# A long network on one core: the pair mask and the conditioning vectors computed inside the expert stage, spline tables in one 128-row stack, zeroing issued at the start

## The reference, cut to what matters

```python
x = x + L0_gnn(layernorm(x), src, dst, ...)    # edge messages, summed over the edges of a node
x = x + L0_ffn(layernorm(x))                   # 64 experts with spline tables, one expert for each node
x = x + L1_gnn(layernorm(x), edge_index, node_vec1, ...)  # 4 blocks of attention over the edges
x = x + L1_ffn(layernorm(x))
```

```python
h = einsum('nd,nhd->nh', xf, Wd[tidx]);  hn = sigmoid(h);  idx = clip(int(hn * 16), 0, 15)
hs = spline_bases[tidx][..., idx] + spline_slopes[tidx][..., idx] * (hn * 16 - idx)
y = einsum('nh,ndh->nd', hs, Wu[tidx]) * scale[tidx]
```

```python
ph = noise_levels * freqs                       # 32 frequencies
cond = silu(concat([sin(ph), cos(ph)]) @ f_w1 + f_b1) @ f_w2 + f_b2    # 16 values for each node
```

## Time and profile before

| | us |
|---|---|
| median of the runs | 3249.67 (3 runs, 3239.88 to 3250.24) |
| the profiled execution | 3248.55 |
| its span in the trace | 3246.8 |

### The profile page before, as it was taken

One profiled execution on the slowest core, in us unless ns is written; L12 is line 12 of the kernel. 1 busy time (PEld: TensorE's weight loads), 2 busy tenths in 40 slices (PEclk: granted clock), 3 DMA queues, 4 the chain that ended last, 5 costly groups with the idle time before them and its releaser, 6 DMA issues. The chain is left out here.

```text
span 3246.8 us, 39720 instructions
## 1 busy us (share of the span) xinstructions
PE 2617.4 (81%) x13663; PEld 2223.8 (68%) x13663; DVE 1904.5 (59%) x3591; ACT 1358.5 (42%) x2707; POOL 1107.7 (34%) x826
## 2 busy tenths in 40 slices
PE   3999998358870178998889988989978999773999
PEld 3688886247670067886678876868866789653997
DVE  1899997624605445776536765457655467625762
ACT  1556664300351234664336653346543356412431
POOL 2788886856701001223103231022311122322520
PEclk9999999668595579999899998999999999985999
DMA  7444442167157411103211012121022210223101
GB/s 223 90 84 78 85 80 52 9 185 186 13 204 201 135 38 48 40 9 95 91 41 56 16 56 88 61 55 40 29 83 78 61 32 17 83 84 89 51 20 32
DMA packets 182808, 245.03 MB, mean 75 GB/s; under 512 B 110073, under 2 KB 118708, under 8 KB 175247
## 3 DMA queue, kind: packets, MB, share of 16 engines
q1 hardware_dynamic: 95852, 213.89, 22.7%
q0 software_dynamic: 86752, 28.51, 5.3%
HBM read 188.85 MB, written 52.95 MB: 74 GB/s over the span
## 5 line engine op out<-in xcount | busy, mean ns | idle before, releaser
L2108 POOL TENSOR_SCALAR prob<-prob,rden,linked 125x1250 f32<-125x1250 f32 x160 | 223.9, 1399 | 959.9 <-DVE rden L2075 959.9
L581 POOL DMA_INDIRECT pairs<-late_cnt,late_idx x160 | 348.0, 2175 | 115.5 <-issue 68.3
L2026 ACT CAST prob_high<-ps 125x375 fp32r<-125x375 f32 (+1 forms) x480 | 231.3, 504 | 266.5 <-PE ps L1988 266.2
L2067 DVE CUSTOM_DVE_ANT_0 prob<-ps,mask 125x1250 f32<-125x1250 f32 x160 | 233.1, 1457 | 128.1 <-PE ps L1964 113.0
L2080 DVE TENSOR_TENSOR prob_low<-ps,prob_high 125x375 fp32r<-125x375 f32 (+1 forms) x480 | 269.7, 585 | 46.6 <-ACT prob_high L2026 46.6
L340 POOL DMA_INDIRECT Hg<-h_rows,dsti x160 | 232.2, 1451 | 102.3 <-issue 82.4
L1977 PE MATMUL ps<-ident,prob 125*125 125x125 f32 x1600 | 252.3, 273 | 17.3 <-POOL prob L2108 10.7
L1977 PEld LDWEIGHTS ps<-ident,prob 125*125 125x125 f32 x1600 | 232.3, 187 | 29.8 <-POOL prob L2108 22.9
L540 PE MATMUL ps<-onehot,mhi 125*128 125x512 f32 (+1 forms) x960 | 245.7, 364 | 6.3 <-DVE onehot L428 5.7
L540 PE MATMUL ps<-onehot,mlo 125*128 125x512 f32 (+1 forms) x960 | 238.5, 357 | 0.0
L2018 ACT ACTIVATE prob<-prob,top 125x1250 f32<-125x1250 f32 x160 | 214.6, 1341 | 44.4 <-DVE top L2067 35.9
(11 more groups left out here) (396 smaller groups left out, 6066.1 us busy)
## 6 DMA issues: line engine op xcount, KB each, us to landing
mask<-mask_d SPq DMA_DIRECT2D x40, 546.9 KB
g_row<-g_d SPq DMA_DIRECT2D x80, 250.0 KB
g_d<-g_row SPq DMA_DIRECT2D x70, 250.0 KB
sg_wd<-L_ffn_Wd SPq DMA_DIRECT2D x32, 512.0 KB
w_ring<-L_ffn_Wd SPq DMA_DIRECT2D x16, 1024.0 KB, 5.3
w_ring<-L_ffn_Wu SPq DMA_DIRECT2D x16, 1024.0 KB, 4.9
pairs<-zeros POOLq DMA_DIRECT2D x18, 625.0 KB, 17.7
keyrow<-keys_d SPq DMA_DIRECT2D x40, 244.1 KB
```

Source lines behind the costliest of these rows:

```text
L581: nc.gpsimd.indirect_dma_start(pairs[a][:, :], bass.IndirectOffsetOnAxis(T.E.late_idx[:, c:c + 1], 0), T.E.late_cnt[:, c:c + 1], None, com ...
L2026: s.copy(M.pt[0][:, n % 3, 0:w], T.ps[0:P, 3 + n % 4, 0:w]).then_inc(high, 1)
L2067: v.tensor_tensor_reduce(M.prob[:, r, :], S(u)[0:P, 0:N], M.mask[:, it % MASKS, :], 1.0, 3.0e38, ALU.add, ALU.min, M.top[:, r:r + 1]).then ...
L2108: nc.gpsimd.tensor_scalar(M.prob[:, r, :], M.prob[:, r, :], M.rden[:, r:r + 1], T.linked[:, it:it + 1], ALU.mult, ALU.mult).then_inc(norme ...
```

## The change

- `pair_mask` and `condition` are no stages any more; their work is written into the lists of `experts`.
- The conditioning: loads by SP behind the tables' load; angles by DVE between down blocks 13 and 25; transposes on PE after down block 34, products after blocks 42 and 56; ACT's part after the rounding of the tables.
- The pair mask: loads and stores are issued by POOL, after the last pair add and after `hs_ready` has reached its last tile; POOL's gathers of `y_d` come behind them. DVE makes the ten tiles after the look-up, with one `tensor_tensor_reduce` in place of the addition and the maximum. ACT takes the logarithms of tiles 0 to 6 after up blocks 12, 20, ... 60, and those of tiles 7 to 9 after the copies of the out phase. Those ten copies are now all ACT's. Two buffers as before.
- The tables: loaded twice, into rows 0 to 63 and 64 to 127. Rows 0 to 63 keep the rounded part, rows 64 to 127 become the rest. `R.hot` has 128 rows with both halves alike (`route` makes them with one more small product), so that a chunk takes 2 matmuls. The last picks of a tile are three over both tables in place of six.
- The zeros are issued without waiting for `x` and the edge inputs.

The diff, cut to its core:

```diff
@@ input_projection, POOL
                     nc.gpsimd.memset(ones33[:], 1.0).then_inc(cleared, 1)
-                    pool.wait_ge(x_in, 32)
-                    pool.wait_ge(e_in, 160)
                     for a in pairs:
@@
+LN0, LNSTEP, LNS = 12, 8, 7
@@ route, PE / ACT / DVE
+                    pe.wait_ge(sec_ready, 1)
+                    pe.wait_ge(doubled, 2)
+                    mm(T.ps[:, 7, 0:4], twice[:].rearrange("p a e -> p (a e)"), sec[:], start=True, stop=True).then_inc(ends_made, 1)
+                    for k in range(2):
+                        nc.scalar.copy(twice[:, k, :], T.ident[0:NX, 0:NX]).then_inc(doubled, 1)
-                    do(v.tensor_scalar(lo_ok[:], T.iota_n[0:NX, :], sec[:, 0:1], None, ALU.is_ge))
+                    dve.wait_ge(ends_made, 1)
+                    do(v.tensor_copy(ends[:], T.ps[:, 7, 0:4]))
+                    do(v.tensor_scalar(lo_ok[:], T.iota_n[:], ends[:, 0:1], None, ALU.is_ge))
@@ experts, SP
-                    sp.dma_start(raw.rearrange("e k g h -> e (k g h)"), tables).then_inc(tab_in, 16)
+                    for part in range(2):
+                        sp.dma_start(raw[part * NX:(part + 1) * NX].rearrange("e k g h -> e (k g h)"), tables).then_inc(tab_in, 16)
+                        sp.dma_start(noise[:], A["node_vec1"].rearrange("(t p) a -> p (t a)", p=P)).then_inc(c_in, 16)
...
+                    sp.wait_ge(c_made, 4)
+                    for p in range(0, CR, 32):
+                        sp.dma_start(fb3[p:p + CH, :], A["L1_gnn_f_b2"].rearrange("(c a) -> c a", a=1)).then_inc(c_in, 16)
@@ experts, POOL
+                    g.iota(fr[:], [[1, NF]], 1, 0, allow_small_or_imprecise_dtypes=True).then_inc(c_made, 1)
+                    g.memset(fb3[:], 1.0).then_inc(c_made, 1)
+                    g.memset(fw3[:], 0.0).then_inc(c_made, 1)
+                    g.memset(T.cw[:], 0.0).then_inc(c_made, 1)
                     late_adds(pool, nc, T, pairs, 3)
                     for s in T.pair_added:
                         pool.wait_ge(s, ET * 8)
+                    pool.wait_ge(hs_ready, NS_T)
+                    for t in range(NT):
+                        if t >= 2:
+                            pool.wait_ge(l_ready, t - 1)
+                        wide(g, pc[:, t % 2, :], counts[0][t * P:(t + 1) * P, :], pc_in[t % 2])
+                        wide(g, pm[:, t % 2, :], counts[1][t * P:(t + 1) * P, :], pc_in[t % 2])
+                        if t >= 1:
+                            pool.wait_ge(l_ready, t)
+                            wide(g, mask_d[(t - 1) * P:t * P, :], pl[(t - 1) % 2], pst[(t - 1) % 2])
+                    pool.wait_ge(l_ready, NT)
+                    wide(g, mask_d[(NT - 1) * P:NT * P, :], pl[(NT - 1) % 2], pst[(NT - 1) % 2])
                     pool.wait_ge(y_stored, 16 * NS_T)
@@ experts, PE
-                        for part in range(2):
-                            for u in range(2):
-                                g = 4 * c + 8 * u
-                                ins = mm(T.ps[:, 2 * (q % 3) + u, :], R.hot[:, t * 128:(t + 1) * 128],
-                                         tab[:, part, a, g:g + 4, :].rearrange("e g h -> e (g h)"), start=part == 0, stop=part == 1)
+                        for u in range(2):
+                            g = 4 * c + 8 * u
+                            ins = mm(T.ps[:, 2 * (q % 3) + u, :], R.hot[:, t * 128:(t + 1) * 128],
+                                     tab[:, a, g:g + 4, :].rearrange("e g h -> e (g h)"), start=True, stop=True)
...
+                        if b == 34:
+                            turn_angles()
+                        if b == 42:
+                            cond_in()
+                        if b == 56:
+                            cond_out()
@@ experts, ACT
+                    act.wait_ge(tab_in, 32)
+                    s.copy(tab[:], raw).then_inc(tab_high, 1)
+                    act.wait_ge(sin_s, 1)
+                    s.activation(emb, ang.rearrange("p t k f -> p t (k f)"), ACT.Sin).then_inc(sin_s, 1)
...
+                        if b >= LN0 and (b - LN0) % LNSTEP == 0 and (b - LN0) // LNSTEP < LNS:
+                            logarithm((b - LN0) // LNSTEP)
-                    for t in range(0, NS_T, 2):
+                    for t in range(NS_T):
                         act.wait_ge(y_turned, t + 1)
                         s.copy(ysb[:, t, :], T.ps[:, 4 + t % 4, :]).then_inc(yc_act, 1)
+                    for t in range(LNS, NT):
+                        logarithm(t)
@@ experts, DVE
-                            for a in range(2):
-                                chain.step(v.copy_predicated(sel[:, u, a, 0:w, :], mask(k, t).broadcast_to([128, w, HID]),
-                                                             sel[:, u, a, w:2 * w, :]))
-                            chain.settle()
+                            do(v.copy_predicated(sel[:, u, :, 0:w, :], mask(k, t).unsqueeze(1).broadcast_to([128, 2, w, HID]),
+                                                 sel[:, u, :, w:2 * w, :]))
-                            v.tensor_tensor(tab[:, 1, :, :, :], raw, tab[:, 0, :, :, :].bitcast(F32),
+                            v.tensor_tensor(tab[NX:128], raw[NX:128], tab[NX:128].bitcast(F32),
                                             ALU.subtract).then_inc(tab_low, 1)
+                        if b == NOVER + 4:
+                            dve.wait_ge(c_made, 4)
+                            dve.wait_ge(c_in, 112)
...
+                    for t in range(NT):
+                        u = t % 2
+                        dve.wait_ge(pc_in[u], 64 * (t // 2 + 1))
+                        if t >= 2:
+                            dve.wait_ge(pst[u], 32 * (t // 2))
+                        v.tensor_tensor_reduce(pc[:, u, :], pc[:, u, :], pm[:, u, :], 1.0, 0.0, ALU.add, ALU.max,
+                                               top[:, t:t + 1]).then_inc(big, 1)
+                        dve.wait_ge(big, 2 * t + 1)
+                        v.tensor_scalar(pl[u], pc[:, u, :], 1.0, None, ALU.max).then_inc(floor, 1)
+                        v.tensor_scalar(pm[:, u, :], pc[:, u, :], 0.5, BIG, ALU.is_lt, ALU.mult).then_inc(big, 1)
+                        dve.wait_ge(big, 2 * t + 2)
+                        dve.wait_ge(logd, t + 1)
+                        v.tensor_tensor(pl[u], pm[:, u, :], pl[u], ALU.subtract).then_inc(l_ready, 1)
@@ second_graph_net
-        pair_mask(nc, T, pairs, mask_d)
-        condition(nc, T, A, T.condT, T.cw)
```

More of the change, by code:

```diff
@@ L877, in _ @@
                        start=True, stop=True).then_inc(over_made, 1)
+                @block.scalar
+                def _(act):
+                    for k in range(2):
+                        nc.scalar.copy(twice[:, k, :], T.ident[0:NX, 0:NX]).then_inc(doubled, 1)
                 @block.vector
@@ L962, in group_loaded, with experts @@
     return n
-def experts(nc, T, A, R, xs_d, y_d, pairs):
+def experts(nc, T, A, R, xs_d, y_d, pairs, mask_d):
     with ExitStack() as ctx:
@@ L976, in experts @@
         tables = A["L0_ffn_splines"].rearrange("e k g h -> e (k g h)")
+        flat = sel[0:P].rearrange("p a b c d -> p (a b c d)")
+        pc = flat[:, 0:2 * N].rearrange("p (u n) -> p u n", u=2)
+        pm = sb("pm_m", [P, 2, N])
+        pl = (flat[:, 2 * N:3 * N], r[0:P].rearrange("p t h -> p (t h)")[:, 0:N])
+        top = sb("pm_top", [P, NT])
+        counts = [a[0:N * N, :].rearrange("(n m) a -> n (m a)", m=N) for a in pairs]
+        rows = xs[:].rearrange("p t d -> p (t d)")[0:P]
@@ L1061, in down, with turn_angles, cond_in, cond_out @@
                         ins.then_inc(made, 1)
+                    def turn_angles():
+                        pe.wait_ge(sin_s, 2)
+                        for t in range(NT):
+                            ins = nc.tensor.transpose(T.ps[0:2 * NF, (0, 1, 6)[t // 4], t % 4 * P:(t % 4 + 1) * P], emb[:, t, :],
+                                                      T.ident[0:P, 0:P])
+                        ins.then_inc(c_turned, 1)
+                    def cond_in():
+                        pe.wait_ge(c_copied, 3)
+                        for c, (n0, nn) in enumerate(CHUNKS):
+                            mm(T.ps[0:CH, (7, 0, 1)[c], 0:nn], fw1[:], embT[:, n0:n0 + nn], start=True, stop=True).then_inc(c_prod, 1)
+                    def cond_out():
+                        pe.wait_ge(c_z, 6)
+                        for c, (n0, nn) in enumerate(CHUNKS):
+                            pe.wait_ge(c_h, c + 1)
+                            mm(T.ps[0:CR, (6, 7, 0)[c], 0:nn], fw3[:], hc[:, n0:n0 + nn], start=True, stop=True).then_inc(c_prod, 1)
                     def chunk(q):
@@ L1258, in expert_layer @@
             route(nc, T, A, xf, sc, xs_d, R, pairs)
-        experts(nc, T, A, R, xs_d, y_d, pairs)
+        experts(nc, T, A, R, xs_d, y_d, pairs, mask_d)
 H, DH = 4, 128
```

259 lines of the change are left out of this document (97 added, 162 removed).

## The result

| | before | after |
|---|---|---|
| median of the runs, us | 3249.66 (4 runs) | 3168.92 (4 runs, 3164.88 to 3176.09) |
| ratio, 95% interval | | 0.9761 (0.9734 to 0.9787) |
| the profiled execution | 3248.55 | 3176.09, its span 3174.4 |

The same kernel run again gave a median of 3174.28, 15.3 above the prediction.

The account below looks back on a forecast made before the run. Stages run in line between barriers, so a removed one is worth its whole length. Terms: -117.8 + 31 - 3 = -89.8 on 3248.55 gives 3158.8; with the median 1.1 above that execution, 3159, whole range 3138 to 3186.

Parts of the forecast that it names:

- Zeros: First stage: zeros issued at once fill only gaps in the transfers, 4.2 us; a gain of 3 taken, 6 either way.
- The experts: Expert stage with mask and conditioning written in: last addition at 1023.2 on the old clock, 31 us later than before.
- Down phase: Expert stage's first products: PE's new work 7 us and a gap grown by 3, sum +10, between 6 and 16.
- Look-up: Experts' table look-up: half the matmuls, DVE then the bound at about 6.1 us a tile; -17 in all.
- First mask load: POOL, after its last pair add has landed: first load of the mask issued at 886 (882 to 891).
- Landing: Mask loads beside the up weights: 9 us (6 to 13) taken from issue to landing, 7.1 before.
- Rounds: Up phase, from one logarithm to the next: 10.7 us taken, between 9.2 and 13.0; first to second 9.8.
- The rival in which the transfers add up: Up phase: weight and mask transfers add to a round of 13.0 us; total 3172, chance 0.12.
- The rival in which the mask hides well: Up phase: rounds of 9.2 us, landing in 7, POOL free at 882, zeros worth 6; total 3142, chance 0.17.
- Tail: After the out copies (983.7): last mask tiles in a line to 1002.7, then gathers to last addition, 20.5 us.
- The rival of POOL held up by DVE: Mask loop: POOL cannot issue transfers while DVE works, 20 to 30 us over seven tiles; total 3185, chance 0.08.
- The starved `x`: First stage: `x` lands at 40 beside the zeros, stage ends about 85 and loses 4 to 10; 3168, chance 0.07.

Follow-up runs that it names:

- no_cond: The changed kernel with the conditioning left out (loads, angles, transposes, products) and its vectors filled with table values; 3168.49 us (1 run), down phase 107.0 us.

## Why the prediction held, and where its steps were off

The change took the two stages out (117.8 predicted; 116.3 between the last addition and `plain_norm`), and the median came out 9.9 us from the forecast. Within that sum, two terms were wrong by more than they were given, and they went opposite ways.

**Zeros: -11.3 in place of -3.** The step that failed is "an earlier start can only fill the gaps: 0.12 x 25 + 0.03 x 40". It took the busy share for the rate. The rows had the rate beside it, 195 and 316 GB/s, and (316 - 195) x 25 us / 316 GB/s = 9.6 us would have come out of them. The rule of the Trainium skill (DMA: Bandwidth & Descriptors, section Queues, rings and completion order), that a transfer engine alternates between its queues packet by packet, stood against this edit. `x` did come later, by 4.3 us, but a loss of 6 did not follow.

**The experts: +53.5 in place of +31.** Counted from the memset, point by point:

| point | predicted | after |
|---|---|---|
| down phase over | 111.1 | 117.7 |
| first up product | 189.6 | 201.3 |
| first mask load | 199 | 206.8 |
| first logarithm | 212.7 | 221.8 |
| seventh logarithm | 276.0 | 299.3 |
| up copies over | 288.5 | 311.3 |
| first gather | 315.7 | 338.1 |
| last addition over | 336.2 | 358.7 |

- *Down phase*: 17 and not 10. It was the upper end of the range and a little more; by no_cond about 11 of it come with the conditioning and 6 without. "PE's gap behind them grows by 3" was too little: the tables were 3.5 us later than before, and the gap went from 3.6 to 8.1. DVE's angles cost at most little in this row: PE waited for DVE's copies eight times, 15.9 us in all, of which one time, 8.1, is the tables', and before it was seven times, 9.3 us, with 3.6 for the tables. Without the tables' wait that is 7.8 against 5.7.
- *Look-up*: -12 (95.5 to 83.6 from first sigmoid to first up product) and not -17. A tile took 6.65 and not 6.1: the pick of 1024 values took 1.36 us on average in place of 1.25, the wait for the fourth chunk was 0.77, and the granted clock was 0.61.
- *First mask load*: 8 us late. The last pair add started 11.8 us later after the memset than before (202.5 and 190.7). POOL did 31 of its 66 adds before the first sigmoid, and 28 before, in a down phase that was 17 us longer; between 677 and 812 it waited 52.6 us for adds to land, and 44.1 before.
- *Landing*: 10.4 us from the end of tile 0's last issue (890.7) to its addition, 9 taken; for tile 2, whose last load was issued by 909.7, behind a store, it was 20.4, beyond the 13 at the upper end. The one-pass sum and maximum took 1.46 + 0.08 us, as taken.
- *Rounds*: 12.9 and not 10.7, with 77.5 us for six in place of 63.3. This is the largest of the wrong terms. The rival in which the transfers add up, with 13.0, was the right one; it had 0.12. Its total, 3172, lies 3.1 and 2.3 us from the two medians of the changed kernel, and the forecast's 9.9 and 15.3. Its own argument from the busy shares gave the number. The rival in which the mask hides well had the byte sum, 88 us for the weights and seven tiles, but took it for room from 876 on; from the first mask load to the seventh logarithm it was 92.5. "20 blocks of weights are loaded ahead" is true and doesn't help: the head start is used up in two and a half rounds, and the phase's seven rounds have to move all that comes after. ACT didn't wait 9 us once, at the first logarithm, but 3.4 there and 6.4 at most later, 27.0 in all over the up phase.
- *Tail*: 21 us from the last copy to the first gather, 19 predicted; gathers and additions 20.5, as predicted. What the prediction didn't say is that tile 7 needn't have been in it.

The rival of POOL held up by DVE fell as a price, though its mechanism shows itself once: of POOL's 40 mask loads two took 1.01 and 0.72 us, at 1002.7 and 1003.7, beside DVE's two scalar passes of 1002.8 to 1004.3; all others took 0.52 to 0.63, and POOL issues them when DVE has just finished a tile. By the rule of the Trainium skill (SBUF — State Buffer, section Who interferes with whom), that VectorE in a two-port mode holds up what GpSimd issues, this is what is to be seen. The trace agrees in these two issues; it cost 0.7 us in all. The starved `x` fell too.

So the total was right partly by luck. Against the forecast of the span, the zeros were off by -8.3 and the experts by +22.5, with +1.5 at the removed stages and -4.2 and +5.9 elsewhere: 17.4 us for the profiled execution. Chance in the unedited stages makes some 6 us of any sum. The second median, 3174.28, lies above the 3148 to 3170 that the forecast had given as its own range.

The signs that the prediction named bear this out. The stage between the last addition and `plain_norm` is gone, as it said. But the stage after the zeros began at 69.9, not 75 to 84; a look-up tile took 6.65, not 6.1; the mask's loads went out 206.8 after the memset, where 882 to 891 is 195 to 204; ACT's wait at its first logarithm was 3.4, not 5 to 12; four of the six distances between logarithms are over 13; and the first gather came at 1019.8, not near 1000.

What stays open: whether the mask could be begun before the pair adds end. The two arrays are read whole, so every add must have landed, and no run here tried another order of the adds.

## What to carry to other kernels

When transfers are laid beside other transfers, count bytes and divide by the rate of the busiest window: the busy share hides how much a window can still take (0.86 busy at 195 GB/s took 155 more), and two phases that are each half full still add up when both are moved into one. A cover has to be read to its end: 5 us of the look-up and a free queue gave nothing here, because the next piece of work hung on another engine's last add, and a down phase that was 11 us shorter gave 6 to 8, while more of the weights came in ahead of the mask. And where an engine makes helper steps inside its main loop, write in as many of them as are ready in time: the one that was left out cost 5 us behind the loop's end.

## What the runs showed of the hardware

- A load of 1250 pieces of 4 bytes took 0.7 us to issue, and the issue of the load behind it on the same queue took 15.6 us, and 0.8 where the pieces were not ahead of it. Given to another engine's queue, the pieces still came with a delay of the tables' 2 MB, issued 14.5 us later on SP's queue, by 5 us; the weights ran beside them too, and no run tells the two apart.
- In the look-up 80 matmuls took 628 ns each by the median, and twice as many took 393 ns each: the granted clock over the look-up was 0.61 and 0.87. In the kernel before, with 160 matmuls over 64 rows, it was 0.50.
- Two transfer issues of POOL beside scalar passes of DVE took 1.01 and 0.72 us, and 0.52 to 0.63 without that company.
- With the zero writes issued into it, a window of 25 us moved 350 GB/s at a busy share of 0.96; without them it moved 195 GB/s at 0.86 and 0.88.
